# The prologue of a fused attention layer: bias products, loads and weight splitting put in another order

## The reference

```
xn  = layernorm(x) * ln_w + ln_b
q   = softmax over each head's 32 channels of (xn @ Wq + bq)
k   = softmax over the 64 tokens of (xn @ Wk + bk - 1e6 * (1 - mask))
v   = (xn @ Wv + bv) * mask
att = k^T v for each head; y = q att
scale, shift = split(silu(cond) @ W_emb + b_emb)        # cond is 128 x 512, W_emb 512 x 512
h   = layernorm(y) * ln2_w + ln2_b, times (1 + scale), plus shift
out = x + silu(h) @ W_out + b_out
```

## Time and profile before

| | before |
|---|---|
| median of 3 runs | 322.28 us (321.87 to 325.95) |
| profiled execution | 323.25 us, its span 321.4 us |
| TensorE busy | 308.0 us, 96% of the span |
| VectorE busy | 275.1 us, 86% |
| GpSimd busy | 229.4 us, 71% |
| ScalarE busy | 193.0 us, 60% |
| mean granted TensorE clock | 0.992 |

### The profile page before, as it was taken

How to read it: one execution, slowest core, us unless ns; L and a number is a source line. 1 busy time by engine, 2 the same in 40 slices (tenths; PEclk the granted TensorE clock), 3 DMA queues, 4 the chain that set the end, 5 groups by cost and what they waited for, 6 DMA issues and landing times.

```text
span 321.4 us, 14568 instructions
## 1 busy us (share of the span) xinstructions
PE 308.0 (96%) x5664; PEld 263.4 (82%) x5664; DVE 275.1 (86%) x749; ACT 193.0 (60%) x378; POOL 229.4 (71%) x276
## 2 busy tenths in 40 slices
PE   7899989999999999999999999999999999999974
PEld 6577867887988898988888898988889898988864
DVE  3775989889797998989898989989898989988883
ACT  1449384667486575668485675757575765756360
POOL 2170459778778687878887787878788887889550
PEclk9999999999999999999999999999999999999979
DMA  7930301050412204040403214050403110010023
GB/s 213 353 110 0 100 4 37 2 167 4 130 38 72 92 8 155 2 163 0 131 32 97 66 42 121 0 163 0 145 19 119 44 65 0 12 55 2 4 68 131
DMA packets 21706, 23.84 MB, mean 74 GB/s; under 512 B 1073, under 2 KB 19121, under 8 KB 21682
## 3 DMA queue, kind: packets, MB, share of 16 engines
q1 hardware_dynamic: 20192, 21.89, 22.0%
q10 hardware_dynamic: 1490, 1.62, 1.5%
HBM read 15.12 MB, written 8.39 MB: 73 GB/s over the span
## 4 chain that ended last, share of the span: by engine, by line
PE 82%; DVE 7%; DMA 4%; issue 2%; ACT 1%; POOL 1%; SPq 1%; POOLq 1%; DVEq 0%
PE bv L890 27%; PE bk L890 27%; PE by L890 13%; PE by L966 4%; PE by L945 4%; PE bv L957 4%; PE by L1026 4%; DMA x_all<-in_x 4%; DVE ystat L769 1%; DVE xstat L621 1%; DVE y_s L760 1%; DVE xt_lo L789 1%; DVE k_t L800 1%; ACT xhat L550 1%; POOLq L45 1%
## 5 line engine op out<-in xcount | busy, mean ns | idle before, releaser
L349 POOL TENSOR_TENSOR k_t<-k_t,kmax 128x512 f32<-128x512 f32 x32 | 34.4, 1074 | 26.3 <-DVE kmax L804 26.3
L496 ACT ACTIVATE k_t<-k_t 128x512 f32<-128x512 f32 x32 | 20.0, 626 | 44.5 <-POOL k_t L349 44.5
L267 POOL TENSOR_TENSOR z_s<-z_s,mod_shift 128x512 f32<-128x512 f32 x30 | 30.7, 1043 | 14.2 <-DVE z_s L720 14.2
L360 POOL TENSOR_TENSOR h_lo<-h_s,h_hi 128x512 fp32r<-128x512 f32 x30 | 38.5, 1306 | 2.9 <-ACT h_hi L513 2.3
L368 POOL TENSOR_TENSOR x_all<-x_all,bo_all 128x1024 f32 (+1 forms) x16 | 38.9, 2434 | 0.0
L550 ACT ACTIVATE xhat<-x_all,xr 128x256 f32 (+1 forms) x62 | 32.2, 591 | 4.6 <-DVE xr L632 3.1
L416 POOL TENSOR_SCALAR y_s<-y_s,yr 128x256 f32<-128x256 f32 x60 | 32.7, 558 | 2.5 <-POOL yr L413 2.2
L800 DVE SCALAR_TENSOR_TENSOR k_t<-off,bk 128x512 f32<-128x512 f32 x32 | 21.9, 683 | 14.5 <-PE bk L890 14.5
L890 PE MATMUL bv<-w_o_hi,h_hi 128*128 128x256 f32 x120 | 32.3, 288 | 0.0
L890 PE MATMUL bv<-w_o_lo,h_hi 128*128 128x256 f32 x120 | 32.2, 290 | 0.0
L520 ACT ACTIVATE xt_hi<-by 128x512 fp32r<-128x512 f32 x32 | 17.4, 597 | 23.4 <-PE by L1026 23.4
(11 more groups left out here) (128 smaller groups left out, 867.2 us busy)
## 6 DMA issues: line engine op xcount, KB each, us to landing
x_all<-in_x SPq DMA_DIRECT2D x15, 512.0 KB, 4.6
out<-x_all SPq DMA_DIRECT2D x15, 512.0 KB, 3.2
off<-in_mask_rows SPq DMA_DIRECT2D x16, 256.0 KB, 3.3
x_all<-in_x SPq DMA_DIRECT2D x2, 256.0 KB, 3.7
z_s<-in_w_emb ACTq DMA_DIRECT2D x1, 512.0 KB, 9.7
h_s<-in_w_emb ACTq DMA_DIRECT2D x1, 512.0 KB, 12.3
out<-x_all SPq DMA_DIRECT2D x2, 256.0 KB, 2.6
y_s<-in_wk ACTq DMA_DIRECT2D x1, 256.0 KB, 3.8
```

The lines of the kernel that those rows point to most:

```text
L267: return eng.tensor_tensor(z, z, mod_shift[:, c, span(g, GB)].unsqueeze(2).broadcast_to([P, GB, SEQ]), ALU.add)
L349: nc.gpsimd.tensor_tensor(kk, kk, kmax[:, c, :].unsqueeze(2).broadcast_to([P, GB, SEQ]), ALU.subtract).then_inc(ksub_d, 1)
L360: nc.gpsimd.tensor_tensor(h_lo[:, c, :], h_s[:, c, :], h_hi[:, c, :].bitcast(fp32), ALU.subtract).then_inc(hlo_d, 1)
L496: nc.scalar.activation(k_t[:, parity, c, :], k_t[:, parity, c, :], ACT.Exp).then_inc(kexp_d, 1)
```

## The change

Five things. (1) The bias product of q and v is issued right behind K's and takes the place of seven dummy products, of which two remain. (2) The loads of cond and W_emb go from ScalarE's queue to SP's, behind x of group 1 and mask 0; x of group 1 goes ahead of mask 0; in ScalarE's queue the bias row goes ahead of W_k. (3) `emb_products` goes behind the four q/v tiles of turn 0, and the `emb` copies of ScalarE to the end of its turn 0. (4) W_k is scaled before `first_xr`, and its high part is rounded by ScalarE (`weights_k_high`) ahead of ScalarE's turn -1. (5) VectorE's turn 0 is: low part of x, `weights_qv`, both mask additions, statistics of group 1, both maxima, `silu_cond`; ScalarE rounds the high part of q/v before the mask and tanh, and does `k_exp` of half 0 behind v tile 3.

```diff
@@ SP's loads
-            load_off(0, 0)
             load_x(1, 1)
+            load_off(0, 0)
+            sp.dma_start(cond[:, :, :], cond_t.rearrange("(c p) b -> p c b", p=P)).then_inc(cond_in, 16)
+            for n in range(2):
+                sp.dma_start(w_e[n][:, :, :], w_emb[n * 2 * P:(n + 1) * 2 * P, :]
+                             .rearrange("(c p) n -> p c n", p=P)).then_inc(we_in, 16)
             sp.dma_start(w_o, w_out.rearrange("(c p) n -> p c n", p=P)).then_inc(wo_in, 16)
@@ ScalarE
             act.dma_start(small[:, :], columns_in).then_inc(small_in, 16)
+            act.dma_start(brow[:, :], b_qvk[None, :]).then_inc(brow_in, 16)
             act.dma_start(w_k, wk.rearrange("(c p) n -> p c n", p=P)).then_inc(wk_in, 16)
-            act.dma_start(brow[:, :], b_qvk[None, :]).then_inc(brow_in, 16)
-            (cond and the two halves of W_emb)
+            def weights_k_high():
+                act.wait_ge(wk_scaled, 1)
+                nc.scalar.activation(w_k_hi[:, :, :], w_k, ACT.Copy).then_inc(wk_high, 1)
...
                     if isinstance(i, int) and i == 0:
+                        weights_qv_high()
                         mask_offset(0, 0)
                         tanh_cond()
...
-                if F:
+                if F and not (isinstance(i, int) and i == 0):
                     k_exp(i, par, 0)
...
-                    if isinstance(i, int) and i == 0:
-                        weights_qv_high()
-                        act.wait_ge(emb_done, 1)
-                        (the four emb copies)
                     v_tile(i, par, 0)
                     v_tile(i, par, 1)
...
                     v_tile(i, par, 2)
                     v_tile(i, par, 3)
+                    if isinstance(i, int) and i == 0:
+                        k_exp(i, par, 0)
                     if not last_turn(i):
                         k_exp(i, par, 1)
                 if N and not (isinstance(i, int) and i < 0):
                     mask_offset(i + 1, 1 - par)
+                if isinstance(i, int) and i == 0:
+                    act.wait_ge(emb_done, 1)
+                    (the four emb copies)
...
+            weights_k_high()
             act.wait_ge(small_in, 16)
             steps(act, body, tail)
@@ VectorE
-                link(last)
-            def weights_k_split():
-                split(w_k, w_k_hi, w_k_lo)
+                last.then_inc(wk_scaled, 1)
+            def weights_k_low():
+                dve.wait_ge(wk_high, 1)
+                nc.vector.tensor_tensor(w_k_lo[:, :, :], w_k, w_k_hi[:, :, :].bitcast(fp32),
+                                        ALU.subtract).then_inc(weights_ready, 1)
...
             def after_first():
+                weights_k_scaled()
                 first_xr()
-                weights_k_scaled()
-                weights_k_split()
+                weights_k_low()
...
                 if isinstance(i, int) and i == 0:
+                    weights_qv()
+                    k_masked(0, 0, 0)
+                    k_masked(0, 0, 1)
+                    x_stats(1, 1)
+                    k_max(0, 0, 0)
+                    k_max(0, 0, 1)
                     silu_cond()
-                    x_stats(1, 1)
-                for c in range(C):
-                    (for F: mask addition, then maximum, of half c)
+                elif F:
+                    for c in range(C):
+                        k_masked(i, par, c)
+                        k_max(i, par, c)
...
-                if isinstance(i, int) and i == 0:
-                    weights_qv()
@@ TensorE
             beta(bk_[0], w_k, 2 * D, D)
-            warm(7)
+            pe.wait_ge(wqv_in, 32)
+            beta(bv_[0], w_qv, 0, 2 * D)
+            warm(2)
...
                     if isinstance(i, int) and i == 0:
-                        pe.wait_ge(wqv_in, 32)
-                        beta(bv_[0], w_qv, 0, 2 * D)
-                        emb_products()
                         pe.wait_ge(weights_ready, 2)
                     qv_tile(i, 0)
                     qv_tile(i, 1)
...
                     qv_tile(i, 2)
                     qv_tile(i, 3)
+                    if isinstance(i, int) and i == 0:
+                        emb_products()
```

More of the change, by code:

```diff
@@ L155, in build_layer @@
         weights_ready = sem("weights_ready")
+        wk_scaled = sem("wk_scaled")
+        wk_high = sem("wk_high")
         wqv_scaled = sem("wqv_scaled")
@@ L533, in body @@
                 if F:
-                    if isinstance(i, int) and i == 0:
-                        weights_qv_high()
-                        act.wait_ge(emb_done, 1)
-                        for j in range(2 * C):
-                            nc.scalar.activation(emb[:, j, :], be[1][:, j * BATCH:(j + 1) * BATCH], ACT.Identity,
-                                                 scale=0.5, bias=b_e[:, j:j + 1]).then_inc(emb_out, 1)
                     v_tile(i, par, 0)
@@ L562, in body @@
                     mask_offset(i + 1, 1 - par)
+                if isinstance(i, int) and i == 0:
+                    act.wait_ge(emb_done, 1)
+                    for j in range(2 * C):
+                        nc.scalar.activation(emb[:, j, :], be[1][:, j * BATCH:(j + 1) * BATCH], ACT.Identity,
+                                             scale=0.5, bias=b_e[:, j:j + 1]).then_inc(emb_out, 1)
             def y_hat(t):
@@ L714, in q_tiles, with k_masked, k_max @@
                                             ALU.subtract).then_inc(qsub_d, 1)
+            def k_masked(i, par, c):
+                wait(dve, k_d, 2 * i + c + 1)
+                wait(dve, off_d, i + 1)
+                if c == 0:
+                    wait(dve, ekt_d, 2 * i - 2)
+                nc.vector.scalar_tensor_tensor(k_t[:, par, c, :], off[:, par, :], -1000000.0, bk_[c][:, :],
+                                               ALU.mult, ALU.add).then_inc(kadd_d, 1)
+            def k_max(i, par, c):
+                wait(dve, kadd_d, 2 * i + c + 1)
+                wait(dve, ksub_d, 2 * i + c - 1)
+                nc.vector.tensor_reduce(out=kmax[:, c, :],
+                                        in_=k_t[:, par, c, :].rearrange("p (b s) -> p b s", s=SEQ),
+                                        axis=AX.X, op=ALU.max).then_inc(kmax_d, 1)
             def z_scaled(g):
@@ L791, in body @@
                 if isinstance(i, int) and i == 0:
-                    silu_cond()
-                    x_stats(1, 1)
-                for c in range(C):
[L795 to L806, removed]
+                    weights_qv()
[4 more added lines that the diff above has]
+                    k_max(0, 0, 1)
+                    silu_cond()
+                elif F:
+                    for c in range(C):
+                        k_masked(i, par, c)
+                        k_max(i, par, c)
                 if O:
```

2 lines of the change are left out of this document (1 added, 1 removed).

## The result

The changed kernel takes 330.56 us (median of 4 runs, 328.05 to 331.26) against 323.0 us before (4 runs, 321.87 to 325.95): a ratio of 1.0206, 95% interval 1.0117 to 1.0295. It is slower, by about 7 us; whether by more than 2% the interval leaves open. 322.1 with a range of 320.2 to 324.0 had been forecast. The ratios leave out executions more than 1.5% above the fastest of their kernel and the medians do not; where such executions may be the effect itself, I give the single times too.

What follows compares the result with a forecast made beforehand. TensorE, busy 59.44 of 60 us from 60 us on, passes on any shift of group 1's K products. Profiled 323.25 us less 0.15 gained gives 323.1; with the median 0.97 lower, 322.1, range 320.2 to 324.0.

Steps and rivals of the forecast that it cites:

- Part 1: Prologue up to the K products: W_k lands at 5.6, transposes of x start at 10.84, 1.20 us later.
- The clock rival: TensorE idles 1.8 us behind 27.0, the clock falls, group 1's transposes and K products lose 1.65 us: 323.8; chance 0.15.
- The fourth rival: W_k or W_v lands a microsecond late, TensorE waits before K's transposes, turn 0 slips: +1 us, 323.1; chance 0.05.
- Part 2: Turn 0's q/v tiles start at 16.3, 5.3 us earlier; tiles and emb_products behind them end at 25.9.
- The head start of 5.3 us: Turn 0's q/v tiles start at 16.3 instead of 21.64; 1.4 us left on TensorE alone at turn 1's transposes.
- Part 3: Into turn 1: ScalarE's queued exponentials and emb copies hold TensorE until 28.8; mask addition only 0.15 us earlier, at 31.55.
- its two bounded terms: Terms bounded rather than read: W_k's landing, -0.6 to +0.6 us, and GpSimd's xr steps, -0.3 to +0.4.
- The reading of the middle: From 60 us on TensorE is busy 59.44 of 60 us, so a shift at turn 1 moves the end equally.

Runs made afterwards that it cites:

- e2: The changed kernel with 13 instead of 7 dummy products ahead of K's bias product; 322.84 us, ratio 1.0000 to before.
- e9: The changed kernel with ScalarE's loads in the order bias row, W_k, small columns; 328.11 us, one run.
- e10: The changed kernel with ScalarE's loads as columns, a wait for GpSimd's memsets, W_k, bias row; 326.22 us, one run.
- e5: The changed kernel with W_k issued ahead of the bias row and 9 instead of 7 dummies ahead of K's bias product; 323.92 us, ratio 1.0034.
- e12: e6 without the last two dummies, group 1's statistics, xr and xhat moved earlier, the k_exp ahead of and behind v tile 2; 321.67 us, ratio 0.9960.
- e1: The changed kernel with W_k issued ahead of the bias row in ScalarE's queue; 326.0 us, ratio 1.0078.
- e6: e5 with the emb copies made by VectorE instead of ScalarE; 322.37 us, ratio 0.9973.
- e11: e1 with 2 instead of 7 dummies ahead of K's bias product; 327.41 us, ratio 1.0169.
- e4: The kernel before with only the q/v bias product moved behind K's, two dummies in place of seven; 327.36 us, ratio 1.0175.
- e3: The kernel before with one edit, the bias row issued ahead of W_k; 326.05 us, ratio 1.0102.
- e8: The changed kernel with W_k, then the bias row, placed behind ScalarE's first activation; W_k's issue still went out at 1.28; 321.58 us, one run.

## Why the prediction was wrong

**Part 1 failed, in two places.** The smaller: W_k's landing, 5.6 with bounds 5.0 and 6.2, was 7.43, which cost 2.0 us. I shifted the issue by 0.6 and kept 3.8 us of transfer as if it went with the load; behind W_q's issue it was 4.4 to 5.9. One row of a queue's order is no bound for another order. The larger: I took the durations of K's and q/v's bias products from rows at full rate, 1.86 and 2.86, without asking what had brought TensorE to that rate. After the change they took 3.13 and 5.71; with the dummies and transposes behind them the rate cost 5.0 us, a term that the sum had at nothing. The same kernel's first 14 dummies, at 0.24 us each, stood in the timeline; the row of 0.49 us of idle time behind them was the margin, and the change pushed it to 2.54.

**The clock rival named the clock, and was wrong in place, way and price.** I looked for a fall behind 27 us, at 1.65 us, chance 0.15. That form exists (e2, e9, e10), but in the profiled execution of the change it did not happen: after a gap of 1.86 us turn 1 ran at full rate. At the front the level was low before the wait already, and that cost 5.0 us, since it stayed low for 12 us of uninterrupted work. Half of 3.3 us was my picture of the price, taken from the one fall in the tail. Nor is there one idle time from which it is decided, as I took: 1.86 us was followed by either level.

**The fourth rival named the late load** but priced it at the wait alone, 1 us, at a chance of 0.05; its sign, transposes of x later than 11.8, came with 17.42. W_v was late too in some traces: it took 4.7 to 6.3 us where I kept 4.9, and TensorE waited 0.64 us for it in e5 and 1.25 in e12.

**Part 2 held from the K products on.** From them to the q/v tiles: 4.19 us against 4.03; tiles and `emb_products`: 9.27 against 9.57. The 0.30 is a misreading: I ended `emb_products` at 21.01, where ScalarE's copies start; the products take 3.57 us, not 3.87. The head start of 5.3 us is real where the front is undisturbed: in e1 the tiles start at 15.87 against 21.64.

**Part 3 held.** TensorE waits for the `emb` copies, 1.86 us, at the place named; ScalarE's order eats the head start. The gain was sized too small: e1's mask addition is 1.1 us earlier than before where 0.15 had been worked out, 0.34 of the difference from the front and 0.60 from the chain behind the K products. e6, which takes the copies away, gains another 0.8. A slip of the sum changes nothing: its two bounded terms add up to -0.9 and +1.0, not to -1.0 and +0.9.

**The reading of the middle held:** a shift of the first mask addition of turn 1 is found again at the last mask addition within 1.8 us, and at the end of the span within 3.4 us, between traces.

The Trainium skill ("TensorE: Matmul & The Clock Gate", Part 1) has sustained activity lift the clock and idleness bring it back. The traces agree with its direction: full rate came behind the 26 dummy instructions of e2 and not behind the four of e11, and the level fell behind waits in e2, e4, e9, e10 and e12.

They do not show that uninterrupted work lifts the level soon. It stayed low through 12.4 us of such work in the changed kernel, 8.6 in e3 (7.81 to 16.4), about 7 in e11 (5.34 to 12.4) and in e9 (7.02 to 13.6). Nor does the kind of product explain it. In the changed kernel nearly all of that work was plain fp32 products, but in e3 fourteen dummy instructions and eight transposes, all on the identity, ran at half rate as well, and in e9 and e11 the level rose while plain fp32 products ran. Even for one order the rise moves: the first 18 dummy instructions take 4.17 us in e5 and 3.71 in e6. Why it came so late in the changed kernel stays open; the measurement decides.

## What to carry to other kernels

Before you take work out of TensorE's start, ask which rate the products behind it have and what gave it to them: dummies ahead of the first product are part of its price, and here waits of 1.25 to 2.54 us behind them went with 1.7 to 5.0 us of lost rate: 5.0 in the change, and in e10 and e12 1.7, by which q/v's bias product took longer than the 3.0 us of e1 and e8. Never take a duration from the prologue without the spacing of equal products beside it; the clock column read 1.00 there at either rate. When moving an issue in one DMA queue, look at what the other queue issues at that moment.

## What the runs showed of the hardware that was not expected

- TensorE stayed at its lower level through 12.4 us of gapless work (the changed kernel, 7.56 to 20) that was mostly plain fp32 products; in e10, behind a wait of 1.40 us, the level fell at 8 us, while such products ran.
- Idle times of 1.25, 1.40, 1.86 and 2.03 us were followed by the lower level in e12, e10, e2 and e4; 1.86 us was not in the changed kernel, e1, e8 and e11.
- The granted clock reads 1.00 at the start of a trace, over products that run at half rate (9 to 19 us of the changed kernel).
- The same 256 KB load took 3.8 to 4.1 us to its landing where it was issued by 1.64 us, and 4.4 to 5.9 where it was issued at 1.76 to 1.82, behind another queue's issue.
- A DMA issue of ScalarE goes out under its table load (e8: issue at 1.28, table load from 1.22 to 2.50).
